# A graph layer on one core: look-ups by max_index, an early second gather, and batches of 2, 2, 2, 3 and 4 tiles

## The reference

```python
h = relu(layernorm(x))                                   # (6250, 256)
out1 = segment_sum(edge, dst); out2 = segment_max(edge, dst)
out3 = out1 / max(count, 1)
z = concat([h, out1, out2, out3, u[0]])                  # 256 + 3*96 + 64 columns
y = relu(z @ W1 + b1) @ W2 + b2                          # hidden 1024, out 256
return x + (y + h)
```

## Time and profile before

| | |
|---|---|
| median of three runs | 555.84 us |
| profiled execution, own time | 558.32 us |
| its span | 556.5 us |
| mean granted TensorE clock | 0.979 |
| busy PE / DVE / ACT / POOL | 497.2 / 441.8 / 396.3 / 251.3 us |
| first layer-1 matmul | 51.88 us |
| last layer-2 matmul ends | about 544.9 us |

### The profile page before, as it was taken

The page is one execution under the profiler, slowest core; times in us unless marked ns, Lnnn a source line. Parts: engine busy times, 40 slices in busy tenths (PEclk is TensorE's granted clock), DMA queues, the critical chain, the costliest instruction groups (busy, mean ns, idle before and its releaser), DMA issues.

```text
span 556.5 us, 9144 instructions
## 1 busy us (share of the span) xinstructions
PE 497.2 (89%) x3098; PEld 453.4 (81%) x3098; DVE 441.8 (79%) x795; ACT 396.3 (71%) x1158; POOL 251.3 (45%) x254
## 2 busy tenths in 40 slices
PE   0099776899999999889999999999999999999991
PEld 0048776899999999789888888887888888888991
DVE  4987749998989999798998889869989789692220
ACT  1966797788879797877877868677768987644230
POOL 2457224453646758364663752644736506002021
PEclk9999898999999999889999999999999999999997
DMA  3947323554554546355543461643533405001010
GB/s 101 282 135 208 120 92 92 186 148 143 148 170 125 211 108 224 127 178 173 162 141 115 157 207 51 199 147 96 164 137 127 144 1 177 19 1 39 1 38 19
DMA packets 18838, 71.13 MB, mean 128 GB/s; under 512 B 4571, under 2 KB 5755, under 8 KB 18776
## 3 DMA queue, kind: packets, MB, share of 16 engines
q0 software_dynamic: 15408, 65.72, 37.3%
q1 hardware_dynamic: 3378, 4.79, 2.9%
HBM read 64.09 MB, written 6.85 MB: 127 GB/s over the span
## 4 chain that ended last, share of the span: by engine, by line
PE 77%; DVE 10%; ACT 6%; issue 2%; DMA 2%; another core or an unknown queue 1%; POOL 0%; DVEq 0%; POOLq 0%; ACTq 0%
PE l1ps L660 30%; PE l1ps L664 15%; PE yps L678 15%; PE yps L682 8%; PE l1ps L667 4%; PE tps L643 3%; DVE work L877 2%; ACT cat L433 2%; DVE work L888 2%; ACT work L486 2%; PE tpr L646 2%; DVE work L899 1%; DMA work<-in_dst 1%; ACT inh L522 1%
## 5 line engine op out<-in xcount | busy, mean ns | idle before, releaser
L354 POOL DMA_INDIRECT work<-in_edge_attr,idx x98 | 118.9, 1213 | 188.0 <-DVE work L899 87.7
L495 ACT ACTIVATE hff<-l1ps,b1e 128x512 f32<-128x512 f32 (+2 forms) x120 | 72.7, 606 | 105.9 <-PE l1ps L667 99.3
L660 PE MATMUL l1ps<-inh,w1h 128*128 128x512 f32 (+2 forms) x480 | 117.1, 367 | 12.8 <-ACT inh L522 7.0
L486 ACT ACTIVATE work<-work,mk 128x96 f32<-128x96 f32 x419 | 117.9, 369 | 0.0
L967 DVE TENSOR_TENSOR hl<-hff,hh 128x512 fp32r<-128x512 f32 (+2 forms) x120 | 70.8, 594 | 55.9 <-ACT hh L497 41.8
L660 PE MATMUL l1ps<-inh,w1l 128*128 128x512 f32 (+2 forms) x480 | 112.9, 358 | 0.0
L664 PE MATMUL l1ps<-inl,w1h 128*128 128x512 f32 (+2 forms) x480 | 112.3, 356 | 0.5 <-DVE inl L971 0.5
L888 DVE TENSOR_TENSOR work<-work 128x384 f32<-128x384 f32 (+9 forms) x154 | 110.5, 739 | 1.2
L373 POOL DMA_INDIRECT out_y<-xr,oidx x49 | 70.4, 1436 | 77.0 <-DVE xr L998 63.0
L678 PE MATMUL yps<-w2h,hh 128*128 128x256 f32 x392 | 99.9, 285 | 0.0
L678 PE MATMUL yps<-w2l,hh 128*128 128x256 f32 x392 | 98.5, 282 | 0.0
(11 more groups left out here) (165 smaller groups left out, 575.2 us busy)
## 6 DMA issues: line engine op xcount, KB each, us to landing
work<-in_L_gnn_W SPq DMA_DIRECT2D x2, 1024.0 KB, 6.0
work<-in_edge_attr,idx POOLq DMA_INDIRECT x98
xr<-in_L_gnn_W SPq DMA_DIRECT2D x1, 1024.0 KB, 11.0
xr<-in_x,nid POOLq DMA_INDIRECT x49
out_y<-xr,oidx POOLq DMA_INDIRECT x49
work<-in_dst SPq DMA_DIRECT2D x1, 415.0 KB
dstp<-in_dst SPq DMA_DIRECT2D x1, 415.0 KB
hff<-in_L_gnn_W SPq DMA_DIRECT2D x3, 128.0 KB, 7.4
```

The source lines that it names most:

```text
L354: pool.indirect_dma_start(out=runs[:, j * k * F:(j + 1) * k * F], out_offset=None, in_=edge, in_offset=bass.IndirectOffsetOnAxis(ap=idx[:, ...
L486: last = act.activation(es[g % 2][:, at * F:(at + 1) * F], run2(g)[:, at * F:(at + 1) * F], ACT.Copy, scale=mk[:, a + j, e:e + 1])
L495: act.activation(hf[C % 2][:, 0:cols], l1ps[C % 2][:, 0:cols], ACT.Relu, bias=b1e[:, m:m + 1])
L660: pe.matmul(ps, wt[:, c, ks(m)], inh[b % 2][:, c, 0:cols], start=(c == 0 and wt is w1h), stop=False)
```

## The change

- **Look-ups.** The window is copied to float32 twice (once on each of VectorE and ScalarE, 1050 elements). ScalarE writes eight thresholds behind a stretch of the copy, and VectorE's `max_index` finds the first place of each of the eight: 7 such instructions over 232, 323, 359, 395, 431, 431 and 329 elements (2500 in all) take the place of the 50 counts. Two small VectorE operations of the threshold set-up and one behind the counts go.
- **Weights.** GpSimd's cast and subtraction go. ScalarE casts all of W1, and TensorE makes 14 low pieces, not 10. The bias products stand after piece 10, the flag's product after piece 8. `WARM` is 20.
- **Second group.** Its runs and its x rows are gathered before GpSimd waits for the flag. Batch 1's tiles take places 2 and 3 of `cat`, so they need not wait for batch 0. Half of its masking goes from ScalarE to VectorE (`masks(1, 1, 1)`).
- **Trees in levels.** `tree_level` is one level of a tree; in batch 0, levels of group 1 stand between `lo` of the chunks. `overlap(late)` stands before the first tree; the two residuals of the first batches and three mask operations (`light_masks`) stand later.
- **Batches.** 16 batches of 2, 2, 2, 3 (five), 4 (six), 2 and 2 tiles.

```diff
-    BATCHES = [[(4, 5)], [(6, 7)], [(8, 9), (44,)], [(10, 11), (45,)], [(12, 13), (46,)], [(14, 15), (47,)], [(16, 17), (48,)],
-               [(18, 19), (42, 43)], [(20, 21), (40, 41)], [(22, 23), (38, 39)], [(24, 25), (36, 37)], [(26, 27), (34, 35)],
-               [(28, 29), (32, 33)], [(0, 1), (2, 3)], [(30, 31)]]
+    BATCHES = [[(4, 5)], [(6, 7)], [(8, 9)], [(10, 11), (44,)], [(12, 13), (45,)], [(14, 15), (46,)], [(16, 17), (47,)], [(18, 19), (48,)],
+               [(20, 21), (42, 43)], [(22, 23), (40, 41)], [(24, 25), (38, 39)], [(26, 27), (36, 37)], [(28, 29), (34, 35)],
+               [(30, 31), (32, 33)], [(0, 1)], [(2, 3)]]
...
-    WARM = 52
+    WARM = 20
...
-            pool.wait_ge(w1a_in, 16)
-            pool.tensor_copy(w1h[:, 0:2, :], raw1[0]).then_inc(w_pool, 1)
-            pool.wait_ge(w_pool, 1)
-            pool.tensor_tensor(out=w1l[:, 0:2, :], in0=raw1[0], in1=w1h[:, 0:2, :], op=ALU.subtract).then_inc(w_pool, 1)
...
+            pool.wait_ge(low_ps, W1A_LOWS)
+            gather_run2(1)
+            gather_run1(1)
+            gather_x(1, list(range(width(1))))
             pool.wait_ge(flag_ready, 1)
...
-            pool.wait_ge(w_pool, 2)
-            gather_run2(1)
-            gather_run1(1)
...
+            act.activation(dwf[0][:, 0:WIN], dw[:, :], ACT.Copy).then_inc(widened, 1)
+            act.wait_ge(widened, 2)
+            for r in reversed(range(LOOKS)):
+                if r + 2 < LOOKS:
+                    act.wait_ge(looked, LOOKS - r - 2)
+                end = sum(part(r))
+                act.activation(dwf[r % 2][:, end:end + 8], thr[:, 8 * r:8 * r + 8], ACT.Copy).then_inc(needles, 1)
...
+            V.tensor_copy(dwf[1][:, 0:WIN], dw[:, :]).then_inc(widened, 1)
+            dve.wait_ge(thr_ready, 1)
+            for r in reversed(range(LOOKS)):
+                lo, w = part(r)
+                dve.wait_ge(needles, LOOKS - r)
+                V.max_index(found[:, 8 * r:8 * r + 8], thr[:, 8 * r:8 * r + 8], dwf[r % 2][:, lo:lo + w + 8]).then_inc(looked, 1)
...
+            act.wait_ge(w1a_in, 16)
+            act.activation(w1h[:, 0:2, :], raw1[0], ACT.Copy).then_inc(w_hi, 1)
+            act.wait_ge(w1b_in, 16)
+            act.activation(w1h[:, 2:4, :], raw1[1], ACT.Copy).then_inc(w_hi, 1)
+            low_parts(0, 2)
+            act.wait_ge(w1r_in, 48)
+            act.activation(w1r[:, :], raw1r[0:3 * KR, :], ACT.Copy).then_inc(w_hi, 1)
+            low_parts(2, 4)
+            act.wait_ge(w2_in, 16)
+            act.activation(w2h[:, :, :], raw2, ACT.Copy).then_inc(w_hi, 1)
+            low_parts(4, 8)
             sums(0)
+            low_parts(8, 10)
             squares(0)
+            low_parts(10, len(LOWS))
+            mask(1, 0, 2)
             norm(0, 0)
...
+            overlap(late).then_inc(mask_ready, 1)
             tree_head(0)
             V.sem_inc(warm_up, 1)
             tree_mid(0)
             scales(0)
+            dve.wait_ge(bias_ps, 1)
             tree_tail(0)
...
+            masks(1, 1, 1)
             in_low(0, 0)
             in_low(0, 1)
+            tree_head(1)
             lo(0)
-            tree_head(1)
+            tree_mid(1)
             lo(1)
-            tree_mid(1)
+            tree_level(1)
             lo(2)
-            residual(0)
-            scales(1)
+            tree_level(1)
+            tree_level(1)
             lo(3)
             tree_tail(1)
+            scales(1)
             lo(4)
+            tree_head(2)
+            lo(5)
+            lo(6)
+            in_low(1, 0)
+            in_low(1, 1)
+            lo(7)
```

More of the change, by code:

```diff
@@ L72, in gnn_block, with place, before_in_place @@
     XS = 4
-    WARM = 52
+    WARM = 20
     def width(b):
         return len(t_of[b])
-    def before_in_slot(b, k):
-        older = [c for c in range(b) if width(c) > k]
-        return t_of[older[-1]][k] if older else None
+    def place(b, k):
+        return k + (2 if b == 1 else 0)
+    def before_in_place(b, at):
+        older = [c for c in range(b) if place(c, 0) <= at < place(c, width(c))]
+        return t_of[older[-1]][at - place(older[-1], 0)] if older else None
     SC = 850
@@ L90, in gnn_block, with part, margin @@
     MEAN = NE // N
-    def part(q):
-        w = 160 if q <= 8 else 232 if q <= 24 else 304
-        return max(0, MEAN * q + STEP // 2 - w // 2), w
-    assert max(sum(part(q)) for q in range(PER + 1)) <= WIN
-    ON_ACT = list(range(1, 45, 2))
-    ON_DVE = [q for q in range(PER + 1) if q not in ON_ACT]
+    LOOKS = -(-(PER + 1) // 8)
+    def part(r):
+        first, last = 8 * r, min(8 * r + 7, PER)
+        def margin(q):
+            return 80 if q <= 8 else 116 if q <= 24 else 152
+        lo = max(0, MEAN * first + STEP // 2 - margin(first))
+        return lo, MEAN * last + STEP // 2 + margin(last) - lo
+    assert max(sum(part(r)) for r in range(LOOKS)) <= WIN
     ROW = 250
@@ L486, in mask @@
                     last = act.activation(es[g % 2][:, at * F:(at + 1) * F], run2(g)[:, at * F:(at + 1) * F], ACT.Copy, scale=mk[:, a + j, e:e + 1])
-                if piece == pieces - 1:
+                if piece == (0 if g == 1 else pieces - 1):
                     last.then_inc(masked, 1)
@@ L594, in _ @@
                         mask(gs[1], 1, 2)
+                    if s == 1 and m in (1, 2):
+                        mask(ahead[0], m, 3)
                     if m == 1 and ahead:
@@ L598, in _ @@
                         squares(b + 1)
-                    if 4 <= m < 7 and ahead:
+                    if 4 <= m < 7 and ahead and s > 1:
                         mask(ahead[0], m - 4, 3)
@@ L632, in _ @@
             last.then_inc(bias_ps, 1)
+            for i in range(W1_LOWS + 2, len(LOWS)):
+                lows(i)
             def transposes(b, k):
@@ L816, in _ @@
             V.tensor_scalar(out=rc[:, :], in0=dg[:, :], scalar1=1.0, scalar2=None, op0=ALU.max)
[L817 to L818 removed]
+            V.tensor_tensor(out=badw[:, 0, :], in0=found[:, 0:PER + 1], in1=wcrow[:, 0:PER + 1], op=ALU.is_ge)
+            first_low = next(8 * r for r in range(LOOKS) if part(r)[0] > 0)
             V.tensor_tensor(out=badw[:, 1, first_low:PER + 1], in0=eloc[:, first_low:PER + 1], in1=lorow[:, first_low:PER + 1], op=ALU.is_le)
@@ L983, in residual @@
                     w = min(2, n - j)
-                    last = V.tensor_tensor(out=xr[:, b % XS, j:j + w, :], in0=xr[:, b % XS, j:j + w, :], in1=cat[:, j:j + w, 0:D], op=ALU.add)
+                    last = V.tensor_tensor(out=xr[:, b % XS, j:j + w, :], in0=xr[:, b % XS, j:j + w, :], in1=cat[:, place(b, j):place(b, j + w), 0:D], op=ALU.add)
                 last.then_inc(dve_step, 1)
```

236 lines of the change are left out of this document (111 added, 125 removed).

## The result

The changed kernel takes **551.06 us** (median of 4 runs, 550.85 to 551.19) where the kernel before took 556.69 in the same rounds: a ratio of **0.9895, with a 95% interval of 0.9853 to 0.9937**. It is faster by 1%, and 11.7 us slower than the 539.4 predicted, outside the stated range of 531 to 550. Its span is 549.3 us; 540.0 was predicted.

What follows compares the result with a forecast made beforehand. TensorE, about 9.46 us a tile, was taken to bound the kernel: start 48.4 + tiles 463.5 + stalls 16.5 + tail 11.6 = 540.0 us span, 539.4 us median after adjustment; range 531 to 550.

Steps and rivals of the forecast that it cites:

- The look-ups: At the start, seven max_index over 2500 elements take 4.5 us and end at 20.4, not 25.6: 5.2 us earlier.
- Flag at 32.9: At the start, the flag stands at 32.9 us, behind eight low weight pieces on TensorE done at 32.1.
- Everything behind the flag: Start: branch 1.63, overlap(late) 1.0, tree 9.97, then 2.85 us to layer 1 at 48.4, 3.5 us gained.
- Clock after 20 warm-ups: TensorE idle from 44 to 46.5 could start batch 0 slow: 1.7 us if it applies, inside the high ends.
- Batch 0: First batch, two tiles: VectorE's list 19.9 us against TensorE's 19.0, stall about 1.5 (0.5 to 6.9).
- batch 1: Second batch, now preparing two tiles: VectorE 17.5 us against 18.9, stall 1.5 for orders between engines (0 to 6.9).
- batch 2: Two tiles preparing three: gets part of batch 1's old stall, 25.5 - 19.5 = 6 us (5 to 12.9).
- rival C: Narrow batches stall from latency, batches 0 to 2 by 6.9, 6.9, 12.9: slower, 559.5 or 563 us; chance 0.09.
- Batches 3 to 6 with the unexplained 2: Three tiles preparing three: stall 1 us in all (0 to 4.4), plus 2 (0 to 5) for stalls without a producer.
- Batch 7: Three tiles preparing four: stall 4.5 us (3 to 5.5), the batch about 33.5 us long.
- batch 14: Near the end, two tiles: batches 13 to 15 cost TensorE 36.8, 18.9, 17.7 us, and VectorE less.
- Rival A: The start gives nothing (W2 slips, ScalarE's list ends later, or the clock falls): 543 to 545 us; chance 0.18.

Runs made afterwards that it cites:

- e13: Changed kernel with the old list of batches, all three early transfers kept, where the kernel before takes 559.1 us: 546.72 us, ratio 0.9789.
- c_after3: The changed kernel once more, unedited, on a chip where the kernel before takes 557.5 us: 552.05 us, ratio 0.9897.
- e11: Changed kernel with all three early transfers of the second group behind the flag, where the kernel before takes 559.1 us: 543.43 us, ratio 0.9728.
- e12: Changed kernel with only one of the second group's three early transfers ahead of the flag, where the kernel before takes 559.1 us: 546.88 us, ratio 0.9796.
- e10: Changed kernel with old batches, one early transfer, flag's product after seven pieces, late overlaps behind first tree, masks between W2's pieces, 30 warm-ups: 538.72 us, ratio 0.9666.

## Why the prediction was wrong

The span missed by 549.3 - 540.0 = 9.3 us: 6.2 at the start, 3.1 in the stalls.

- **The look-ups** were right in kind and 1 us better: done at 19.34, not 20.4.
- **"Flag at 32.9": the step that failed.** The product was made on time and read 6.5 us late. I had weighed the early gathers only for what they take from W2's load (0, high end 2.9), and what came was another cost: on a chip of that sort the signals of TensorE, and some of VectorE's, stood late until the transfers thinned out (e13 and c_after3 against e11 and e12). From product to flag the sum allowed 0.8 us (32.1 to 32.9); it took 7.0 (32.29 to 39.32).
- **Everything behind the flag** (branch 1.28 for 1.63, `overlap(late)`, tree) had about its forecast length.
- **Clock after 20 warm-ups:** inside my high ends, and it happened: first chunks at 0.50. Together with a slower way from tree to layer 1 (3.15 for 2.85) some 1.5 us.
- **Batch 0** 0.5 (1.5 predicted), **batch 1** 3.2 (1.5), **batch 2** 6.1 (6; its own figures give 25.0 - 19.5 = 5.5): 0.8 more in all, and rival C is dead, batch 1 taking 22.1.
- **Batches 3 to 6 with the unexplained 2:** 2.2 for 3 (28.10, 28.45, 29.30, 29.92 against 28.4). The wait that no producer explains was not noise of that execution but came in batches 5 and 6 whenever the new list ran on a late chip, and late signals stand there.
- **Batch 7** 6.0 for 4.5; **batch 14** 1.5 that I had at 0 ("VectorE less"); the batches of four and 13 about as before. The last batch is 0.7 shorter (17.1) and the tail 0.7 longer.
- Rival A's mechanism (W2, ScalarE's list, clock) did not decide, but its outcome, a start that gives nothing, is what happened. The 12.9 and 6.9 of batches 0 and 1 that I let go as stalls of order were in part (batch 0's 4 us) waits of that chip. On a late chip both kernels carry about 8.5 us of such waits, the one before in batches 0 and 5, the changed one at the flag (6.2) and in batches 5 and 6 (2.3); on the quick chips neither has them. So the ratio is much the same on both, 0.990 and 0.986 to 0.988. My forecast counted the waits of before as gained and put nothing in their place: on a late chip they were gained and came back elsewhere, on a quick one they were never there.

Not settled: what in a late chip delays the signals; why the changed kernel's batches 5 and 6 meet it with the new list and not with the old; how much of e10's gain is due to each of its parts.
